# Moving squares of attention probabilities through the device's memory instead of directly between partitions

## The chip, the cores and the metric

The kernel runs on one core of one Trainium2 chip. The metric is the device time of the whole kernel in microseconds (us). The engines are TensorE (PE in the profile, PEld for its weight loads), VectorE (DVE), ScalarE (ACT), GpSimd (POOL) and SyncE (SP), which here only issues transfers. The core has 16 DMA engines.

## The reference

Input is x of 8 x 512 tokens with 128 features, 4096 tokens in all. Three residual steps follow one another: a mixture-of-experts feed-forward, an attention over a memory of 4096 keys, and the same feed-forward again.

```python
x = x + 0.5 * ffn(layernorm(x))       # 8 experts of 176, the best 2 of each token, and a shared one
x = x + attn(layernorm(x))
x = x + 0.5 * ffn(layernorm(x))

# attn (only its first output is used)
q      = h @ Wq.T + bq
scores = q @ memory_keys.T / sqrt(128)        # 4096 tokens x 4096 keys
probs  = softmax(scores)
out    = (probs @ memory_values) @ Wo.T + bo
```

## The kernel before

**Stages.** The first feed-forward takes the time up to about 125 us, the attention from there to about 600 us, the second feed-forward the rest. Each engine has its own program in a fixed order; semaphores alone tie them together.

**Units.** The attention runs over 16 units. A unit is 4 tiles of 128 tokens (512 tokens) against one half of the keys (2048). It is cut into 8 half tiles, each 128 tokens x 1024 keys; the loops call the running number of a half tile H, so that unit u has H = 8u to 8u + 7. For each half tile TensorE computes the scores (`scores`, L1138 to L1140), VectorE their maximum (`maximum`, L909), and ScalarE the exponentials (`exponentials`, L647 or L656).

**Transposing.** The product with the values needs the probabilities transposed, keys on partitions. For one of the 4 tiles of a unit TensorE does this (`transpose_pair`, L1157). The other three (MOVED = 3) are the "moved" tiles: their exponentials are written to the buffer `E2`, VectorE transposes 32 x 32 blocks in place (`transpose_squares`, L904), and DMA carries each square of 32 partitions to the partitions on which it belongs in `probsT`. For a block row b and a source group i of 32 partitions this is one transfer of its own from `E2[i*32:(i+1)*32, ..., b, :]` to `probsT[b*32:(b+1)*32, ...]`. So there are 16 transfers for a batch, and a unit has two batches: tiles 0 and 1 (128 KB each transfer), and tile 2 (64 KB each). `probsT` has two halves, used by turns of units; `E2` has one.

**Splitting and use.** ScalarE copies 768 columns of `probsT` to `p_hi` in fewer bits (`moved_high`, L629), GpSimd subtracts to get `p_lo` (`moved_low`, L423), and TensorE multiplies both with the values (L1178 to L1180). There are 8 such steps ("rings") to a unit. The first `moved_high` of unit u waits until both batches of unit u are in (`moved[0]`, `moved[1]`). In ScalarE's fixed order it stands at H = 8(u + 1) + 2, between the exponentials of half tiles 2 and 3 of unit u + 1.

**Order on SyncE** (L312 to L324). For each unit: wait until the half of `probsT` is free (`moved_lo_done`), then for each batch wait for its transposed squares (`squares_done`) and issue its 16 transfers. The batch of tiles 0 and 1 waits for the squares of half tile 3. VectorE transposes half tile 3 two half tiles later in its own order, after `own_low` (L897) and `maximum` (L909).

**Reuse of E2.** The exponentials of the next unit may write into `E2` only when the batch there has landed (`wait(act, moved[...], moves(u))` in `exponentials`).

Of the kernel before, what the change touches and what calls it, by code (L numbers as in the profile page):

```python
# [4 lines left out]
fp32 = mybir.dt.float32  # L5
# [6 lines left out]
P = 128  # L12
# [4 lines left out]
N = GT * P  # L17
# [24 lines left out]
MOVED = 3  # L42
OWN = GT - MOVED
BATCHES = ((0, 2), (2, 1))
SQ = 32
QUADS = P // SQ
# [26 lines left out]
def macaron_kernel(nc: bass.Bass, x, wup, wdown, gate_w, expert_bias, shared_up, shared_down,  # L73
                   wq, bq, wo, bo, keys_values, out):
    with ExitStack() as ctx:
        def sb(name, shape, dt):
            return ctx.enter_context(nc.sbuf_tensor(name, shape, dt))

        def sem(name):
            return ctx.enter_context(nc.semaphore(name))  # L80
# [31 lines left out]
        E2 = sb("E2", [P, MOVED, QUADS, N], fp32)  # L112
# [12 lines left out]
        probsT = sb("probsT", [P, 2, MOVED * QUADS, KC, SQ], fp32)  # L125
# [22 lines left out]

        p_hi = sb("p_hi", [P, HI_RING, GT * QUADS, 2 * SQ], fp32r)
        p_lo = sb("p_lo", [P, HI_RING, GT * QUADS, 2 * SQ], fp32r)  # L150
        bank_max = sb("bank_max", [P, 2, 2], fp32)
        neg_max = sb("neg_max", [P, 4, GT], fp32)
        row_sum = sb("row_sum", [P, 4, GT, 2], fp32)
# [63 lines left out]
        exp_done = sem("exp_done")  # L217
        probsT_done = sem("probsT_done")
        squares_done = sem("squares_done")
        moved = [sem(f"moved{k}") for k in range(len(BATCHES))]  # L220
        p_hi_done = sem("p_hi_done")
        p_lo_done = sem("p_lo_done")
# [17 lines left out]
        def wait(eng, s, n):  # L240

            if not isinstance(n, int) or n > 0:
                eng.wait_ge(s, n)
# [12 lines left out]
        def score_pair(u, i, h):  # L256

            p = (2 * (u * GT + i) + h) % SCORE_PAIRS
            return banks[:, 2 * p:2 * p + 2, :]
# [17 lines left out]
            return TB[:, 0:2 * OWN * P].rearrange("p (c a q) -> p a c q", c=2, q=SQ)  # L277

        def moves(units):
            return 16 * QUADS * QUADS * units  # L280

        def batch_of(i):
            return [k for k, (first, count) in enumerate(BATCHES) if first <= i < first + count][0]
# [5 lines left out]
        def tiles_of(g):  # L289
            return bass.ds(g * GT, GT)  # L290

        @block.sync
        def _(sp):
            sp.dma_start(X[:, 0:GT, :], x[:, 0:GT, :]).then_inc(x_loaded[0], 16)
            sp.dma_start(wup_f, wup).then_inc(up_w_loaded, 16)
            sp.dma_start(X[:, GT:2 * GT, :], x[:, GT:2 * GT, :]).then_inc(x_loaded[1], 16)
            small = [(sup_s[:, :, :], shared_up), (sdown_s[:, :, :], shared_down), (wq_s[:, :], wq), (bq_s[:, :], bq)]
            for dst, src in small:
                sp.dma_start(dst, src).then_inc(small_w_loaded, 16)
            sp.dma_start(X[:, 2 * GT:3 * GT, :], x[:, 2 * GT:3 * GT, :]).then_inc(x_loaded[2], 16)  # L300
            sp.dma_start(wdown_f, wdown).then_inc(down_w_loaded, 16)
            sp.dma_start(X[:, AHEAD * GT:, :], x[:, AHEAD * GT:, :]).then_inc(x_loaded[AHEAD], 16)
            for b in range(2):
                sp.dma_start(kv_stage[:, b, :], keys_values[:, b, :]).then_inc(kv_loaded[b % 2], 16)
            for dst, src in [(wo_s[:, :], wo), (bo_s[:, :], bo.to_broadcast([P, D]))]:
                sp.dma_start(dst, src).then_inc(out_w_loaded, 16)
            for b in range(2, KV):
                sp.wait_ge(kv_hi_done, b - 1)
                sp.wait_ge(kv_lo_done, b - 1)
                sp.dma_start(kv_stage[:, b % 2, :], keys_values[:, b, :]).then_inc(kv_loaded[b % 2], 16)  # L310

            for u in range(UNITS):  # L312
                if u == 0:
                    sp.wait_ge(z_done, GROUPS)
                    sp.wait_ge(down_done, GROUPS * SLOTS)
                wait(sp, moved_lo_done, UP * (u - 1))
                for k, (first, count) in enumerate(BATCHES):
                    sp.wait_ge(squares_done, 2 * (MOVED * u + first + count))
                    for b in range(QUADS):
                        for i in range(QUADS):  # L320
                            target = probsT[b * SQ:(b + 1) * SQ, u % 2, :, :, :].rearrange(
                                "p (t i) c q -> p i t (c q)", t=MOVED)[:, i, first:first + count, :]
                            sp.dma_start(target, E2[i * SQ:(i + 1) * SQ, first:first + count, b, :]  # L323
                                         ).then_inc(moved[k], 16)  # L324
            for g in range(GROUPS):
                sp.wait_ge(x_updated, GROUPS + g + 1)
                sp.dma_start(out[:, tiles_of(g), :], X[:, tiles_of(g), :]).then_inc(stored, 16)
            sp.wait_ge(stored, 16 * GROUPS)
# [3 lines left out]
        def _(pool):  # L332
# [32 lines left out]
            def spread_weights(G):  # L365

                slots = routed_slots(G)
                T = (slots.stop - slots.start) * GT
                pool.wait_ge(weights_ready, route_event(G) + 1)
                if G == GROUPS:  # L370
                    pool.wait_ge(moved[-1], moves(UNITS))
                if G >= 2:
                    pool.wait_ge(wbc_done, G)
                pool.tensor_copy(wide_weights(G)[:, slots, :].rearrange("p s (m r) -> p (s m) r", r=ROWS),
                                 weight[:, slots, :, :].rearrange("p s t e -> p (s t e)").unsqueeze(2)
                                 .to_broadcast([P, T * E, ROWS])).then_inc(weights_spread, 1)

            def cast_xT(n, G, i):

                pool.wait_ge(xT_copied, n + 1)  # L380
                wait(pool, up_done, SLOTS * (G - AHEAD))
                if G == GROUPS:
                    pool.wait_ge(moved[0], moves(UNITS))
                pool.tensor_copy(xTb[:, i % RING, :], xT[i % RING]).then_inc(xTb_done, 1)
# [99 lines left out]
        def _(act):  # L484
# [138 lines left out]
            def moved_high(ring):  # L623

                if ring % UP == 0:
                    for k in range(len(BATCHES)):
                        act.wait_ge(moved[k], moves(ring // UP + 1))
                wait(act, pv_done, 2 * (ring - HI_RING + 1))
                act.activation(moved_part(p_hi, ring), moved_pair(ring // UP, ring % UP), ACT.Copy  # L629
                               ).then_inc(moved_hi_done, 1)  # L630

            def exponentials(u, i, h):

                v = u % 4
                act.wait_ge(neg_max_done, u * GT + i + 1)
                source = score_pair(u, i, h)
                if u == 0 and i == 0 and h == 0:
                    act.wait_ge(shared_up_done, GROUPS)
                    act.wait_ge(up_done, GROUPS * SLOTS)
                    act.wait_ge(weighted, GROUPS * SLOTS)  # L640
                if i < MOVED:
                    if h == 0:
                        wait(act, moved[batch_of(i)], moves(u))
                        if u == 0 and i == MOVED - 1:
                            act.wait_ge(kv_lo_done, KV)
                    strips = E2[:, i, :, :].rearrange("p b (c q) -> p c b q", q=SQ)
                    act.activation(  # L647
                        strips[:, 2 * h * QUADS:2 * (h + 1) * QUADS, :, :],
                        source.rearrange("p k (c b q) -> p (k c) b q", b=QUADS, q=SQ), ACT.Exp,
                        bias=neg_max[:, v, i:i + 1], accum_out=row_sum[:, v, i, h:h + 1]).then_inc(exp_done, 1)  # L650
                else:
                    if i == MOVED and h == 0:
                        wait(act, probsT_done, (u - 1) * UP)
                        if u < 2:
                            act.wait_ge(ffn_w_cast, 2)
                    act.activation(  # L656
                        probs[:, v % 2, i - MOVED, 2 * h * N:2 * (h + 1) * N],
                        source.rearrange("p b n -> p (b n)"), ACT.Exp,
                        bias=neg_max[:, v, i:i + 1], accum_out=row_sum[:, v, i, h:h + 1]).then_inc(exp_done, 1)
# [22 lines left out]
            for u in range(UNITS + 2):  # L682
                g = u // 2
                prepares = u % 2 == 1 and u < LAST
                for h in range(HALVES):
# [6 lines left out]
                    if u < UNITS:  # L692
                        exponentials(u, h // 2, h % 2)
# [608 lines left out]
```

## Time and profile before

| | us |
|---|---|
| median of 3 runs | 693.62 |
| lowest and highest | 691.54, 698.07 |
| the profiled execution | 697.09 |
| its span, first to last instruction | 695.3 |

| engine | busy us | share of the span |
|---|---|---|
| PE | 617.1 | 89% |
| DVE | 533.2 | 77% |
| ACT | 469.5 | 68% |
| POOL | 392.7 | 56% |

The shares are means over three stages. "SPq" in a row means SyncE's queue of DMA issues, and "issue" as a releaser means that the profile shows nothing the engine waited for. The device's memory was read for 8.12 MB and written for 2.10 MB in the whole run; all DMA together moved 61.17 MB.

### The profile page before, as it was taken

What the parts mean: (1) busy time and instruction counts of PE and PEld (TensorE: products, weight loads), DVE (VectorE), ACT (ScalarE), POOL (GpSimd) and SP (SyncE); (2) the same over time, 40 slices, a digit from 0 to 9 for tenths busy, and PEclk for the clock granted to TensorE, in tenths of its full rate; (3) what the DMA queues carried; (4) which work ended last, traced back from release to release, by engine and by line L of the source; (5) the groups of instructions that cost most, each with busy time, mean ns of one, the idle gap of its engine ahead of it and who ended that gap; (6) DMA issues with size and microseconds to landing.
All of it is one profiled execution on the core that took longest, in us unless ns stands there. A gap on an engine that the chain in (4) does not pass through costs nothing.

```text
span 695.3 us, 9149 instructions
## 1 busy us (share of the span) xinstructions
PE 617.1 (89%) x2768; PEld 429.7 (62%) x2768; DVE 533.2 (77%) x952; ACT 469.5 (68%) x773; POOL 392.7 (56%) x386
## 2 busy tenths in 40 slices
PE   3898979657998998999999999999999858699997
PEld 2544434535876776877777777777777646454542
DVE  3798876866977977888887897896797645188885
ACT  2477979335776776777776777776776644178886
POOL 4755512024765865867766677686687687542200
PEclk9799999988999999999999999999999988899999
DMA  7002010065364453553653644635526530000001
GB/s 286 2 30 62 30 61 0 8 160 124 73 155 95 115 133 86 139 131 77 156 117 74 152 108 104 145 93 127 133 65 149 120 81 0 1 6 26 31 18 44
DMA packets 37092, 61.17 MB, mean 88 GB/s; under 512 B 9051, under 2 KB 9651, under 8 KB 36915
## 3 DMA queue, kind: packets, MB, share of 16 engines
q1 hardware_dynamic: 36755, 60.57, 34.8%
q8 instruction: 23, 0.38, 0.2%
q14 instruction: 26, 0.21, 0.1%
q10 hardware_dynamic: 288, 0.01, 0.0%
HBM read 8.12 MB, written 2.10 MB: 15 GB/s over the span
## 4 chain that ended last, share of the span: by engine, by line
PE 40%; SPq 22%; DVE 14%; issue 11%; POOL 6%; ACT 6%; DMA 1%; ACTq 0%; DVEq 0%; POOLq 0%
SPq L323 22%; PE banks L1021 4%; POOL p_lo L423 4%; PE banks L1030 3%; PE banks L1138 3%; PE banks L1179 3%; PE banks L1140 3%; PE banks L1139 3%; PE banks L1178 3%; PE banks L1180 3%; DVE probsT L810 3%; PE banks L986 3%; DVE bank_max L909 3%; DVE E L904 2%; PE banks L1037 2%
## 5 line engine op out<-in xcount | busy, mean ns | idle before, releaser
L423 POOL TENSOR_TENSOR p_lo<-probsT,p_hi 128x768 fp32r<-128x768 f32 x128 | 235.4, 1842 | 136.3 <-ACT p_hi L629 135.6
L909 DVE TENSOR_REDUCE bank_max<-banks 128x1 f32<-128x1024 f32 x128 | 155.8, 1217 | 36.3 <-PE banks L1140 35.7
L629 ACT ACTIVATE p_hi<-probsT 128x768 fp32r<-128x768 f32 x128 | 107.9, 843 | 30.1 <-issue 27.2
L1138 PE MATMUL banks<-kv_lo,q_parts 128*128 128x512 f32 x256 | 112.5, 440 | 13.6 <-ACT E L647 10.3
L810 DVE SCALAR_TENSOR_TENSOR probsT<-banks,E 128x1024 bf16<-128x1024 f32 x80 | 95.5, 1219 | 35.3 <-PE banks L1021 31.6
L904 DVE STREAM_TRANSPOSE E<-E 128x1024 f32<-128x1024 f32 x96 | 118.4, 1234 | 4.2 <-ACT E L647 4.2
L647 ACT ACTIVATE E<-banks,neg_max 128x1024 f32<-128x1024 f32 x96 | 106.8, 1113 | 20.7 <-DVE neg_max L915 13.4
L531 ACT ACTIVATE probsT<-probsT 128x1024 bf16<-128x1024 bf16 x96 | 92.2, 980 | 31.8 <-DVE probsT L810 22.9
L1178 PE MATMUL banks<-p_hi,kv_lo 128*128 128x512 f32 x256 | 109.3, 427 | 3.9 <-POOL p_lo L423 3.9
L621 ACT ACTIVATE p_hi<-banks 128x256 fp32r<-128x256 f32 x128 | 49.0, 383 | 82.1 <-PE banks L1157 82.0
L1179 PE MATMUL banks<-p_lo,kv_hi 128*128 128x512 f32 x256 | 103.7, 405 | 0.0
L1180 PE MATMUL banks<-p_hi,kv_hi 128*128 128x512 f32 x256 | 103.6, 405 | 0.0
L1140 PE MATMUL banks<-kv_hi,q_parts 128*128 128x512 f32 x256 | 102.1, 399 | 0.0
L1139 PE MATMUL banks<-kv_hi,q_parts 128*128 128x512 f32 x256 | 102.1, 399 | 0.0
L897 DVE TENSOR_TENSOR p_lo<-banks,p_hi 128x256 fp32r<-128x256 f32 x128 | 52.0, 407 | 56.0 <-ACT p_hi L621 55.8
L1138 PEld LDWEIGHTS banks<-kv_lo,q_parts 128*128 128x128 f32 x256 | 49.0, 192 | 22.1 <-ACT E L647 11.8
L1021 PE MATMUL banks<-E,wup_b 128*128 128x512 bf16 x176 | 54.6, 398 | 8.3 <-ACT probsT L520 6.4
L1178 PEld LDWEIGHTS banks<-p_hi,kv_lo 128*128 128x128 f32 x256 | 49.1, 192 | 16.8 <-issue 5.5
L1180 PEld LDWEIGHTS banks<-p_hi,kv_hi 128*128 128x128 f32 x256 | 49.0, 191 | 12.6
L1179 PEld LDWEIGHTS banks<-p_lo,kv_hi 128*128 128x128 f32 x256 | 48.9, 191 | 12.0 <-issue 2.0
L1030 PE MATMUL banks<-probsT,wdown_b 128*128 128x512 bf16 x176 | 52.5, 386 | 4.3 <-ACT probsT L531 4.2
L1140 PEld LDWEIGHTS banks<-kv_hi,q_parts 128*128 128x128 f32 x256 | 48.7, 190 | 11.6
(101 smaller groups left out, 874.8 us busy)
## 6 DMA issues: line engine op xcount, KB each, us to landing
probsT<-E SPq DMA_DIRECT2D x256, 128.0 KB, 2.4
probsT<-E SPq DMA_DIRECT2D x256, 64.0 KB, 2.0
E<-in_keys_values SPq DMA_DIRECT2D x8, 512.0 KB, 3.4
out<-X SPq DMA_DIRECT2D x8, 256.0 KB, 2.1
X<-in_x SPq DMA_DIRECT2D x1, 1280.0 KB, 8.8
X<-in_x SPq DMA_DIRECT2D x3, 256.0 KB, 5.2
probsT<-in_wup SPq DMA_DIRECT2D x1, 704.0 KB, 6.7
probsT<-in_wdown SPq DMA_DIRECT2D x1, 704.0 KB, 6.2
```

The lines of the kernel that those rows point to most:

```text
L323: sp.dma_start(target, E2[i * SQ:(i + 1) * SQ, first:first + count, b, :]).then_inc(moved[k], 16)
L423: pool.tensor_tensor(moved_part(p_lo, ring), moved_pair(ring // UP, ring % UP), moved_part(p_hi, ring).bitcast(fp32), ALU.subtract).then_i ...
L629: act.activation(moved_part(p_hi, ring), moved_pair(ring // UP, ring % UP), ACT.Copy).then_inc(moved_hi_done, 1)
L810: dve.scalar_tensor_tensor(hidden[:, k, :, :], up_banks[PAIR_BANK[k]], 0.0, spread.unsqueeze(1).to_broadcast([P, 2, N]), ALU.max, ALU.mult ...
L904: dve.transpose(half, half).then_inc(squares_done, 1)
L909: dve.tensor_reduce(bank_max[:, i % 2, h:h + 1], score_pair(u, i, h).rearrange("p b n -> p (b n)"), AX.X, ALU.max).then_inc(bank_max_done, 1)
L1138: pe.matmul(bank, qh, kl, start=True, stop=False)
L1139: pe.matmul(bank, ql, kh, start=False, stop=False)
L1140: pe.matmul(bank, qh, kh, start=False, stop=True).then_inc(scores_done, 1)
L1178: pe.matmul(OB, vl, hi, start=(c == 0), stop=False)
L1179: pe.matmul(OB, vh, lo, start=False, stop=False)
L1180: pe.matmul(OB, vh, hi, start=False, stop=(c == KC - 1)).then_inc(pv_done, 1)
```

## The change

Each batch of moved tiles is first written as a whole, from all 128 partitions, to a new tensor `spill` in the device's memory (one transfer of 2 MB or of 1 MB). SyncE waits until it has landed (`spilled`), then issues four transfers back, one for each block row b, which gather the squares of all source partitions into the 32 partitions of `probsT` (512 KB or 256 KB each). `E2` is released when the transfer out has landed, instead of when the squares have arrived. The amount that arrives in `probsT` is the same. Nothing else changes.

```diff
--- before.py
+++ after.py
@@ -148,6 +148,8 @@
 
         p_hi = sb("p_hi", [P, HI_RING, GT * QUADS, 2 * SQ], fp32r)
         p_lo = sb("p_lo", [P, HI_RING, GT * QUADS, 2 * SQ], fp32r)
+
+        spill = nc.dram_tensor("spill", [2, MOVED, P, QUADS * N], fp32, kind="Internal").ap()
         bank_max = sb("bank_max", [P, 2, 2], fp32)
         neg_max = sb("neg_max", [P, 4, GT], fp32)
         row_sum = sb("row_sum", [P, 4, GT, 2], fp32)
@@ -217,6 +219,7 @@
         exp_done = sem("exp_done")
         probsT_done = sem("probsT_done")
         squares_done = sem("squares_done")
+        spilled = [sem(f"spilled{k}") for k in range(len(BATCHES))]
         moved = [sem(f"moved{k}") for k in range(len(BATCHES))]
         p_hi_done = sem("p_hi_done")
         p_lo_done = sem("p_lo_done")
@@ -277,7 +280,7 @@
             return TB[:, 0:2 * OWN * P].rearrange("p (c a q) -> p a c q", c=2, q=SQ)
 
         def moves(units):
-            return 16 * QUADS * QUADS * units
+            return 16 * QUADS * units
 
         def batch_of(i):
             return [k for k, (first, count) in enumerate(BATCHES) if first <= i < first + count][0]
@@ -316,12 +319,15 @@
                 wait(sp, moved_lo_done, UP * (u - 1))
                 for k, (first, count) in enumerate(BATCHES):
                     sp.wait_ge(squares_done, 2 * (MOVED * u + first + count))
+                    wait(sp, moved[k], moves(u - 1))
+                    place = spill[u % 2, first:first + count]
+                    sp.dma_start(place.rearrange("t p n -> p t n"), E2[:, first:first + count, :, :].rearrange(
+                        "p t b n -> p t (b n)")).then_inc(spilled[k], 16)
+                    sp.wait_ge(spilled[k], 16 * (u + 1))
                     for b in range(QUADS):
-                        for i in range(QUADS):
-                            target = probsT[b * SQ:(b + 1) * SQ, u % 2, :, :, :].rearrange(
-                                "p (t i) c q -> p i t (c q)", t=MOVED)[:, i, first:first + count, :]
-                            sp.dma_start(target, E2[i * SQ:(i + 1) * SQ, first:first + count, b, :]
-                                         ).then_inc(moved[k], 16)
+                        sp.dma_start(probsT[b * SQ:(b + 1) * SQ, u % 2, first * QUADS:(first + count) * QUADS, :, :]
+                                     .rearrange("p i c q -> p i (c q)"), place[:, :, b * N:(b + 1) * N].rearrange(
+                            "t (i p) n -> p (t i) n", i=QUADS)).then_inc(moved[k], 16)
             for g in range(GROUPS):
                 sp.wait_ge(x_updated, GROUPS + g + 1)
                 sp.dma_start(out[:, tiles_of(g), :], X[:, tiles_of(g), :]).then_inc(stored, 16)
@@ -640,7 +646,7 @@
                     act.wait_ge(weighted, GROUPS * SLOTS)
                 if i < MOVED:
                     if h == 0:
-                        wait(act, moved[batch_of(i)], moves(u))
+                        wait(act, spilled[batch_of(i)], 16 * u)
                         if u == 0 and i == MOVED - 1:
                             act.wait_ge(kv_lo_done, KV)
                     strips = E2[:, i, :, :].rearrange("p b (c q) -> p c b q", q=SQ)
```

SyncE's program is the place of the change. These are its rows for two units in the middle before, with the semaphores that each row waits for (`probsT<-E` is a direct transfer of squares; x15 counts equal rows):

```order
19 L323 DMA probsT<-E 32x2x512 [waits squares_done]
20 L323 DMA probsT<-E 32x2x512 x15
21 L323 DMA probsT<-E 32x512 [waits squares_done]
22 L323 DMA probsT<-E 32x512 x15
23 L323 DMA probsT<-E 32x2x512 [waits squares_done,moved_lo_done]
24 L323 DMA probsT<-E 32x2x512 x15
25 L323 DMA probsT<-E 32x512 [waits squares_done]
26 L323 DMA probsT<-E 32x512 x15
```

And the same two units of the change:

```order
27 L324 DMA spill<-E 128x2x2048 [waits moved0,squares_done,moved_lo_done]
28 L328 DMA probsT<-spill 32x8x512 [waits spilled0]
29 L328 DMA probsT<-spill 32x8x512 x3
30 L324 DMA spill<-E 128x2048 [waits moved1,squares_done]
31 L328 DMA probsT<-spill 32x4x512 [waits spilled1]
32 L328 DMA probsT<-spill 32x4x512 x3
33 L324 DMA spill<-E 128x2x2048 [waits moved0,squares_done,moved_lo_done]
34 L328 DMA probsT<-spill 32x8x512 [waits spilled0]
35 L328 DMA probsT<-spill 32x8x512 x3
36 L324 DMA spill<-E 128x2048 [waits moved1,squares_done]
37 L328 DMA probsT<-spill 32x4x512 [waits spilled1]
38 L328 DMA probsT<-spill 32x4x512 x3
```

A unit had 32 issues behind two waits for squares; now it has 10, with two more waits in which SyncE sits until its own transfer out has landed.

ScalarE's program is the place that waits for the moved squares. Before, around the first `moved_high` of a unit (L629) and the exponentials of half tile 3 (the second L647), on which the next unit's first batch depends:

```order
173 L621 ACTIVATE p_hi<-banks 128x256 [waits pv_done,probsT_done]
174 L647 ACTIVATE E,row_sum<-banks,neg_max 128x8x4x32 [waits moved0,neg_max_done]
175 L629 ACTIVATE p_hi<-probsT 128x768 [waits pv_done,moved1,moved0]
176 L621 ACTIVATE p_hi<-banks 128x256 [waits pv_done,probsT_done]
177 L647 ACTIVATE E,row_sum<-banks,neg_max 128x8x4x32 [waits neg_max_done]
```

Of the change:

```order
173 L627 ACTIVATE p_hi<-banks 128x256 [waits pv_done,probsT_done]
174 L653 ACTIVATE E,row_sum<-banks,neg_max 128x8x4x32 [waits spilled0,neg_max_done]
175 L635 ACTIVATE p_hi<-probsT 128x768 [waits pv_done,moved1,moved0]
176 L627 ACTIVATE p_hi<-banks 128x256 [waits pv_done,probsT_done]
177 L653 ACTIVATE E,row_sum<-banks,neg_max 128x8x4x32 [waits neg_max_done]
```

No instruction has moved on ScalarE; the wait of the exponentials is now for the transfer out, and that of `moved_high` is the same as before.

## Rows read from the trace of the kernel before

**Rows 1.** The page: busy time of the engines, and the chain that ended last.

```profile
PE 617.1 (89%) x2768; PEld 429.7 (62%) x2768; DVE 533.2 (77%) x952; ACT 469.5 (68%) x773; POOL 392.7 (56%) x386
...
PE 40%; SPq 22%; DVE 14%; issue 11%; POOL 6%; ACT 6%; DMA 1%; ACTq 0%; DVEq 0%; POOLq 0%
```

**Rows 2.** Waits of ScalarE and of SyncE's queue: total us, times, longest.

```profile
ACT p_hi L629 <- issue: 27.2, 15, 3.5
ACT E L647 <- DMA probsT<-E: 7.3, 2, 6.5
...
SPq L318 <- DVE E L904: 120.3, 15, 35.3
```

**Rows 3.** Lines 323 and 629: duration ns min/median/max, first and last start us.

```profile
L323 SPq DMA_DIRECT2D probsT<-E x512: 507/596/2051, 137.1 to 566.8; - x171
...
L629 ACT ACTIVATE p_hi<-probsT x128: 833/843/858, 159.2 to 590.5; 128x768 fp32r<-128x768 f32 x128
```

**Rows 4.** Timeline of SyncE, units 8 and 9: start us, length us, transfers.

```profile
354.55 21.59 SPq L323 DMA_DIRECT2D probsT<-E  x32
...
381.77 21.86 SPq L323 DMA_DIRECT2D probsT<-E  x32
```

**Rows 5.** Timeline of ScalarE and VectorE between them: start, length, [idle before].

```profile
377.65 0.84 ACT L629 ACTIVATE p_hi<-probsT 128x768 fp32r<-128x768 f32 x1 [2.96 <-issue]
378.40 0.36 ACT L621 ACTIVATE p_hi<-banks 128x256 fp32r<-128x256 f32 x1
378.67 1.11 ACT L647 ACTIVATE E<-banks,neg_max 128x1024 f32<-128x1024 f32 x1
...
378.80 0.42 DVE L897 TENSOR_TENSOR p_lo<-banks,p_hi 128x256 fp32r<-128x256 f32 x1 [1.82 <-ACT p_hi L621]
379.14 1.22 DVE L909 TENSOR_REDUCE bank_max<-banks 128x1 f32<-128x1024 f32 x1
380.39 0.16 DVE L915 TENSOR_REDUCE neg_max<-bank_max 128x1 f32<-128x2 f32 x1
380.46 1.24 DVE L904 STREAM_TRANSPOSE E<-E 128x1024 f32<-128x1024 f32 x1
```

**Rows 6.** The same timelines: squares of tile 2, and the last unit's first L629.

```profile
388.68 1.24 DVE L904 STREAM_TRANSPOSE E<-E 128x1024 f32<-128x1024 f32 x1
...
568.89 0.84 ACT L629 ACTIVATE p_hi<-probsT 128x768 fp32r<-128x768 f32 x1 [3.54 <-issue]
```

**Rows 7.** The page's DMA issues: transfers, KB each, median us from issue to landing.

```profile
probsT<-E SPq DMA_DIRECT2D x256, 128.0 KB, 2.4
probsT<-E SPq DMA_DIRECT2D x256, 64.0 KB, 2.0
E<-in_keys_values SPq DMA_DIRECT2D x8, 512.0 KB, 3.4
out<-X SPq DMA_DIRECT2D x8, 256.0 KB, 2.1
```

**Rows 8.** Windows: length, busy us of PE, PEld, DVE, ACT, POOL, PEclk, DMA share, GB/s.

```profile
10.00:13.00 3.00, 2.22 (x10) 1.78 (x8) 0.00 (x0) 1.86 (x2) 2.92 (x7) 1.00 1.04 434
193.00:203.00 10.00, 9.68 (x49) 7.67 (x48) 7.20 (x10) 6.93 (x14) 6.27 (x4) 1.00 0.88 203
204.00:214.00 10.00, 10.00 (x49) 8.03 (x48) 8.33 (x10) 5.91 (x11) 7.37 (x5) 1.00 0.38 95
300.00:518.00 218.00, 211.49 (x991) 164.88 (x990) 181.98 (x286) 157.53 (x287) 154.05 (x113) 1.00 0.49 116
...
693.60:694.60 1.00, 0.00 (x0) 0.00 (x0) 0.00 (x0) 0.00 (x0) 0.00 (x0) 0.59 0.69 262
```

**Rows 9.** Windows of TensorE alone: length, PE busy us, PEclk, DMA share, GB/s.

```profile
144.20:147.60 3.40, 0.69 (x3) 1.00 0.88 204
147.60:151.00 3.40, 0.33 (x1) 0.51 0.63 149
151.00:154.50 3.50, 3.50 (x9) 0.50 0.39 95
...
374.00:378.00 4.00, 3.60 (x17) 1.00 0.33 82
```

**Rows 10.** The page: traffic with the device's memory over the whole run.

```profile
HBM read 8.12 MB, written 2.10 MB: 15 GB/s over the span
```

## The prediction, as it went on record

> **What bounds the kernel now.** I read the page first. TensorE is busy for 89% of the span, but only 40% of the chain that ended last is PE, and 22% is SyncE's queue of issues [rows 1]. That is too much for an engine which computes nothing, so I looked at what releases what.
>
> SyncE issues 512 direct transfers, from 137.1 to 566.8 us, and one issue takes 596 ns [rows 3]. A unit's 32 follow each other in one string of 21.6 us (unit 8) and 21.9 us (unit 9) [rows 4]. The string starts when VectorE has transposed half tile 3; SyncE waits there 15 times [rows 2]. At the other end ScalarE's first `moved_high` of a unit waits for the last square: "issue", 15 times, 27.2 us in sum, up to 3.5 us at once [rows 2]. The profile names no releaser, but the last landing of unit 8 fits: the string ends at 376.1 us, its last transfer was issued some 0.6 us earlier, a 64 KB transfer lands 2.0 us after its issue [rows 4, 7], which is 377.5, and L629 starts at 377.65 [rows 5].
>
> These two waits close a ring, for the exponentials of half tile 3 stand behind that same `moved_high` in ScalarE's order. The timeline shows it [rows 5]: L629 at 377.65, the copy L621, then VectorE's L897, maximum, and the transpose L904 from 380.46 to 381.70; SyncE's next string starts at 381.77 [rows 4]. So a unit costs D + G. D goes from the first issue to L629, 377.65 - 354.55 = 23.1 us. G goes from L629 to the next first issue, 381.77 - 377.65 = 4.12 us. Check: the first issue is at 137.1, the last unit's L629 at 568.89 [rows 3, 6]; 137.1 + 16 x 23.1 + 15 x 4.12 = 568.5. The ring sets the attention's time; what comes before 137.1 and after 568.9 is not touched.
>
> How much other engines leave below it: in 300 to 518 us, eight units, PE is busy for 211.49 of 218.0 us [rows 8]. That is 26.4 us for a unit of 27.25. So a shorter D gives little, a longer D costs its full length in every unit.
>
> **The change, part by part.** It removes 32 issues from D and puts two round trips in their place, one after the other, since SyncE waits for each transfer out itself.
>
> Rates. Loads over 128 partitions moved 434 GB/s with all 16 DMA engines full (share 1.04), 417 GB/s for a share of 1 [rows 8]. Transfers into 32 partitions moved 203 GB/s at a share of 0.88; with no idle engine that is 231 [rows 8]. Each DMA engine is half as fast there: 434 / 1.04 / 16 = 26 GB/s against 203 / 0.88 / 16 = 14.4. The transfers back also end in 32 partitions each, so I take 217, the middle of 203 and 231. That it is the narrow destination and not the narrow source that costs is my choice; no row of before has one without the other (rival 1).
>
> Fixed parts. The 256 KB store lands after 2.1 us [rows 7], of which 0.63 are data at 417 GB/s: 1.5. The 64 KB transfer lands after 2.0, less 0.30 for data at 217: 1.7. The 512 KB load lands after 3.4, less 1.26: 2.1, the upper end for all.
>
> The new D:
> - Out, batch 0: 1.5 + 2.097 MB / 417 GB/s = 1.5 + 5.03 = 6.5 us.
> - Back, batch 0 (four issues, hidden behind the data of the first), with the transfer out of batch 1 queued behind it on the same DMA engines: 1.7 + 9.66 + 2.51 = 13.9 us. Its squares are no hindrance: half tile 5 is transposed at 389.92, 8.2 us after the string's start [rows 4, 6], and SyncE comes to that issue at 6.5 + 4 x 0.64 = 9.1 us.
> - Back, batch 1: 1.7 + 4.83 = 6.5 us.
> - SyncE waking up twice: 0.1 us, a guess.
>
> D = 27.0 us, against 23.1. If the transfer out of batch 1 is not held back by the one before, its fixed part and wait overlap with data, about 1.8 us less.
>
> What is costed at nothing: G, which has no DMA in it; ScalarE's earlier release of `E2` (at 6.5 instead of about 12 us into the unit). The latter removes at most the 7.3 us of two waits [rows 2], and both lie before an L629 that waits anyway. The longer stall is 27.0 + 4.12 - 26.4 = 4.7 us of a unit, in which PE, DVE and POOL run dry; their work, 26.4 us at most, fits into 31.1. SyncE has no other work in this stage, and the transfers that it would delay are the stores of the last stage, from 624 us on.
>
> Sum: 137.1 + 16 x 27.0 + 15 x 4.12 = 630.9 against 568.9: 62.0 us more. The profiled execution took 697.1 us, 3.5 more than the median of 693.6; it would become 759.1, and the median 755.6.
>
> A page's price for the fixed part: the Trainium skill ("DMA: Bandwidth & Descriptors", Anatomy of one DMA) gives about 2.0 us, most of it the receipt of the write, with the device's memory as the slowest target. As an estimate D would be 1.1 us longer by it, and the median 773. The store's 2.1 us in all [rows 7] speak against so much.
>
> **The rivals.**
>
> *Rival 1, faster: the way back runs at full rate.* If the half rate comes from reading 32 partitions, the transfers back read the device's memory and move at 417 GB/s. Then D = 6.5 + (1.7 + 5.03 + 2.51) + (1.7 + 2.51) + 0.1 = 20.1, below the 22.3 at which the other engines (26.4 - 4.12) become the bound. The gain lies between 8 units x 6.5 us of PE idleness, doubled (13 us), and the 27.2 us of rows 2: about 674 us. The switch is at D = 23.1, a rate back of 3.15 MB / 10.8 us = 291 GB/s. For it: the first loads do reach 434. Against it: they spread over 128 partitions; the rate of an engine fell by almost half as soon as a transfer covered 32. Chance 7%. The Trainium skill ("SBUF — State Buffer", Door 1: The DMA port swizzle) says that 32 partitions reach 8 of 16 ports and at most about 218 GB/s, whichever the other side is; the direct transfers' 203 agree. The same page (The DMA setup-cost knee) has 2 us + bytes / 436 GB/s for wide transfers, with the advice to make one large transfer of many; by that alone this rival would hold, at an estimated D of 20.4.
>
> *Rival 2, much slower: pieces of 2 KB from the device's memory.* The way back gathers 2 KB pieces, 8 KB apart from partition to partition and 256 KB from square to square, while 16 engines run in step. Traffic with that memory goes from 8.12 + 2.10 MB [rows 10] to about 111 MB, and rows show it at full rate for 3 us only; one store over 1 us moved 262 GB/s [rows 8]. With 150 GB/s back (a bound I set between the 95 and 203 of rows 8), D is 33.4 and the median 858. For it: nothing in the trace shows such a gather. Against: the loads of x are 2 KB pieces too. Chance 9%. The Trainium skill ("DMA: Bandwidth & Descriptors", Latency and other measured facts) has copies within that memory at 207 GB/s with a row pitch of 512 KiB and at 103 with 4 MiB; whether a pitch of 8 or 256 KB costs anything no run here shows.
>
> *Rival 3, slower by the clock.* Where PE was busy for only 0.69 of 3.4 us, its clock went from 2.4 to 1.2 GHz for the next 6.9 us [rows 9]; the 3 us stall at 374 to 378 us left it at 2.4. A stall of 4.7 us may drop it. At half speed for 6.9 us PE falls behind by at most 3.5 us, less than 4.7: nothing. Only if it stays low for twice as long, it becomes the bound, at 26.4 + 6.9 = 33.3 us a unit: 2.2 x 16 = 35 us more, 791. Chance 5%.
>
> *Rival 4, no change:* fixed parts and rates err together, so that D falls to 22.5 to 23.5. It needs 4 us less than summed. Chance 3%.
>
> **The numbers.** The forecast of 756 us has 76%. Its own bounds: with 231 and 434 GB/s and 1.5 us each time, D is 25.6 and the median 733; with batch 1's way out overlapped as well, some 24 and 708. With 203, 262 (the store) and 2.1 us each, D is 33.8 and the median 864. Not all go one way, so I take somewhat over half the way on either side, 725 to 815; rival 3 lies within, the others outside. A difference of 1% is about what a measurement of this kernel can tell. Faster by over 1%: 7%, rival 1. Within: 3%. Slower: 90%.
>
> **What would show it.** SyncE's rows: 160 issues in the attention, the read back starting 6 to 8 us after the transfer out. Traffic with the memory of 58 MB read and 52 MB written. The DMA rate on the way back near 217 GB/s. L629's idle time before it (now [rows 5] 2.96 us) at 4 to 7 us in each unit, and the first L629 at 164 us instead of 159.2. PE's busy share in mid-attention down from 97% to about 85%. G still at 4.1 us. I am wrong if the transfers back show much over 217 GB/s or batch 1's transfer out lands before the last square of batch 0, if the idle time is not before L629, or if PEclk falls below 1 for most of the stage.

## The result

| | before, us | the change, us | ratio, 95% interval |
|---|---|---|---|
| median of 4 runs each | 694.75 | 804.96 | 1.158 [1.149, 1.167] |
| span of the profiled execution | 695.3 | 805.9 | |

The change costs 110 us. The forecast was 62 us more (756, range 725 to 815): the direction, the place and the mechanism came out, and the rise that was forecast is just over half of the one measured.

### The profile page after: what moved, and what is told of

Its sections match the earlier page's. It is cut to its first block, busy times and chain, and to the rows that moved or that the text cites. A ratio compares the mean times of both kernels' runs of the same rounds, so it can differ in the third digit from the quotient of the medians.

```text
span 805.9 us, 8811 instructions
## 1 busy us (share of the span) xinstructions
PE 644.3 (80%) x2768; PEld 450.7 (56%) x2768; DVE 536.6 (67%) x952; ACT 467.8 (58%) x773; POOL 391.7 (49%) x386
## 4 chain that ended last, share of the span: by engine, by line
DMA 31%; issue 23%; PE 21%; DVE 13%; POOL 6%; ACT 4%; SPq 3%; ACTq 0%; DVEq 0%; POOLq 0%
DMA spill<-E 30%; PE banks L1027 3%; PE banks L1036 3%; DVE probsT L816 3%; DVE bank_max L915 3%; DVE E L910 3%; SPq L328 3%; POOL p_lo L429 2%; PE banks L1043 2%; PE banks L969 2%; PE banks L992 1%; POOL xn L364 1%; PE banks L984 1%; PE banks L1144 1%; PE banks L1145 1%
## 5 line engine op out<-in xcount | busy, mean ns | idle before, releaser
L635 ACT ACTIVATE p_hi<-probsT 128x768 fp32r<-128x768 f32 x128 | 108.0, 843 | 132.7 <-issue 116.9
L1144 PE MATMUL banks<-kv_lo,q_parts 128*128 128x512 f32 x256 | 115.5, 451 | 11.0 <-ACT E L653 7.7
L1184 PE MATMUL banks<-p_hi,kv_lo 128*128 128x512 f32 x256 | 115.3, 451 | 3.9 <-POOL p_lo L429 3.9
L816 DVE SCALAR_TENSOR_TENSOR probsT<-banks,E 128x1024 bf16<-128x1024 f32 x80 | 95.6, 1218 | 33.5 <-PE banks L1027 29.7
L1185 PE MATMUL banks<-p_lo,kv_hi 128*128 128x512 f32 x256 | 108.5, 424 | 0.0
L1186 PE MATMUL banks<-p_hi,kv_hi 128*128 128x512 f32 x256 | 108.0, 422 | 0.0
L1145 PE MATMUL banks<-kv_hi,q_parts 128*128 128x512 f32 x256 | 104.9, 410 | 0.0
L1146 PE MATMUL banks<-kv_hi,q_parts 128*128 128x512 f32 x256 | 104.6, 409 | 0.0
L627 ACT ACTIVATE p_hi<-banks 128x256 fp32r<-128x256 f32 x128 | 48.9, 382 | 91.8 <-PE banks L1163 91.7
L969 PE MATMUL banks<-ident,xn 128*128 128x128 f32 x96 | 20.7, 354 | 91.7 <-DVE p_lo L903 70.2
L1163 PE MATMUL banks<-ident,probs 128*128 128x128 f32 x256 | 52.9, 290 | 28.7 <-DVE p_lo L903 27.1
L969 PEld LDWEIGHTS banks<-ident,xn 128*128 128x128 f32 x96 | 14.4, 179 | 98.9 <-DVE p_lo L903 73.7
L1163 PEld LDWEIGHTS banks<-ident,probs 128*128 128x128 f32 x256 | 36.3, 149 | 54.5 <-DVE p_lo L903 32.5
L1184 PEld LDWEIGHTS banks<-p_hi,kv_lo 128*128 128x128 f32 x256 | 52.9, 207 | 17.8 <-issue 5.6
```

The costliest lines, as they stand in the source:

```text
L816: dve.scalar_tensor_tensor(hidden[:, k, :, :], up_banks[PAIR_BANK[k]], 0.0, spread.unsqueeze(1).to_broadcast([P, 2, N]), ALU.max, ALU.mult ...
L1144: pe.matmul(bank, qh, kl, start=True, stop=False)
L1145: pe.matmul(bank, ql, kh, start=False, stop=False)
L1146: pe.matmul(bank, qh, kh, start=False, stop=True).then_inc(scores_done, 1)
L1184: pe.matmul(OB, vl, hi, start=(c == 0), stop=False)
L1185: pe.matmul(OB, vh, lo, start=False, stop=False)
```

## The profile after, beside that of before

The page of the change, its parts 1 to 4 in extract (compare [rows 1, 10]):

```profile
span 805.9 us, 8811 instructions
...
PE 644.3 (80%) x2768; PEld 450.7 (56%) x2768; DVE 536.6 (67%) x952; ACT 467.8 (58%) x773; POOL 391.7 (49%) x386
...
HBM read 58.45 MB, written 52.43 MB: 138 GB/s over the span
...
DMA 31%; issue 23%; PE 21%; DVE 13%; POOL 6%; ACT 4%; SPq 3%; ACTq 0%; DVEq 0%; POOLq 0%
```

DVE, ACT and POOL are busy as long as before, within 4 us. PE is busy for 27 us more with the same 2768 matmuls, at a lower granted clock (see e5). The chain has changed its owner: SyncE's issues fell from 22% to 3%, and DMA, 1% before, is now 31%. "issue", which is also the releaser that the profile gives for the wait at the end of the ring, grew from 11% to 23%. Now the waits that the change adds, and the one at the end of the ring (compare [rows 2]; total us, times, longest):

```profile
SPq L328 <- DMA spill<-E: 299.9, 32, 13.6
...
ACT p_hi L635 <- issue: 116.9, 15, 10.1
```

SyncE sits for 300 us in the 32 waits for its own transfers out. ScalarE's wait before the first `moved_high` (L629 before, L635 now) grew from 27.2 to 116.9 us in the same 15 units, by 89.7. One unit in the middle shows the whole ring. These are the timelines of SyncE, ScalarE and VectorE for unit 8 (compare [rows 4, 5]):

```profile
408.81 0.38 SPq L324 DMA_DIRECT2D spill<-E  x1
415.22 1.78 SPq L328 DMA_DIRECT2D probsT<-spill  x4
417.10 0.52 SPq L324 DMA_DIRECT2D spill<-E  x1
431.23 1.73 SPq L328 DMA_DIRECT2D probsT<-spill  x4
...
438.94 0.84 ACT L635 ACTIVATE p_hi<-probsT 128x768 fp32r<-128x768 f32 x1 [9.33 <-issue]
439.69 0.36 ACT L627 ACTIVATE p_hi<-banks 128x256 fp32r<-128x256 f32 x1
439.96 1.11 ACT L653 ACTIVATE E<-banks,neg_max 128x1024 f32<-128x1024 f32 x1
...
440.09 0.42 DVE L903 TENSOR_TENSOR p_lo<-banks,p_hi 128x256 fp32r<-128x256 f32 x1 [8.19 <-ACT p_hi L627]
440.43 1.22 DVE L915 TENSOR_REDUCE bank_max<-banks 128x1 f32<-128x1024 f32 x1
...
441.75 1.24 DVE L910 STREAM_TRANSPOSE E<-E 128x1024 f32<-128x1024 f32 x1
```

The stretch from L635 to the end of the transpose (442.99) is the same as before: G is 4.1 us. D is 438.94 - 408.81 = 30.1 us, where it was 23.1. The three legs of D can be read off SyncE's rows: 6.4 us out, 16.0 us back and out again, 7.7 us back. Over the 16 units the means are 6.65, 15.6 and 7.7, in sum 29.9. The same means before were D = 22.8 and G = 4.5, so that unit 8 with its 23.1 and 4.12 is right in the sum and slightly off in both parts.

The ring accounts for the whole: D rose by 7.16 us in 16 units, and the 15 stretches G between them shrank by 0.39, which makes 108.7 us. The last unit's first L635:

```profile
677.62 0.84 ACT L635 ACTIVATE p_hi<-probsT 128x768 fp32r<-128x768 f32 x1 [8.72 <-issue]
```

It came at 568.89 before [rows 6]: 108.7 of the span's 110.6 us have been lost up to there, and the first transfer left at 137.1 before and at 137.2 now.

The DMA landings of the page (KB each, median us; compare [rows 7]):

```profile
spill<-E SPq DMA_DIRECT2D x16, 2048.0 KB, 6.4
probsT<-spill SPq DMA_DIRECT2D x64, 512.0 KB, 8.5
spill<-E SPq DMA_DIRECT2D x16, 1024.0 KB, 13.0
probsT<-spill SPq DMA_DIRECT2D x64, 256.0 KB, 5.1
```

The 2 MB out land in 6.4 us, and the 1 MB out take 13.0: they stand behind the four transfers back. And windows of SyncE's view, which carry only length, granted clock, DMA share and GB/s, for the legs of unit 8 (compare [rows 8]):

```profile
409.70:414.60 4.90, 0.85 1.03 428
416.10:417.10 1.00, 1.00 0.74 160
417.10:425.90 8.80, 1.00 1.02 212
429.30:431.10 1.80, 1.00 0.04 18
432.10:433.60 1.50, 1.00 0.67 156
433.60:436.80 3.20, 0.73 1.05 228
436.80:438.40 1.60, 0.50 0.27 54
```

In full flow the transfers back move 212 to 228 GB/s, and 217 was assumed. But the second and the third leg each start with 1.0 to 1.5 us at some 160, and end with one or two in which few DMA engines still work. In 429.3 to 431.1 the share is 0.04, less than one engine of 16, and SyncE waits for it.

## The experiments

All runs were compared with the kernel before on the same chip, whose medians there were 696.8 to 698.1 us. Runs on different chips are compared by their ratios to it. D and G are means over the 16 units, if no unit is named.

The theory is the ring: the attention takes 16 D + 15 G, with a floor set by the other engines. Its rivals: traffic with the device's memory as such costs time, or TensorE's lower clock does.

**Transfers back to 128 partitions (e1).**

```diff
-  sp.dma_start(probsT[b*SQ:(b+1)*SQ, u % 2, first*QUADS:(first+count)*QUADS, :, :] ...,
-               place[:, :, b*N:(b+1)*N].rearrange("t (i p) n -> p (t i) n", i=QUADS))
+  row = first * QUADS + b * count
+  sp.dma_start(probsT[:, u % 2, row:row + count, :, :] ...,
+               place[:, :, b*N:(b+1)*N].rearrange("t p n -> p t n"))
```

> The changed kernel, but each of the four transfers back of a batch goes from the same bytes of the spill tensor (2 KB pieces, 8 KB apart) to all 128 partitions, in place of 32; the squares arrive in wrong places, the amount is the same. In the changed kernel a unit's D (first issue to first L629) is 29.9 us and the data back of batch 0 move at 193 GB/s. If the 32 partitions at the destination set that rate: back at over 400 GB/s, D = 6.5 + (1.7 + 5.0 + 2.5) + (1.7 + 2.5) = 20 us, the ring falls below the other engines, 675 to 695 us. If gathering 2 KB pieces from the device's memory sets it: still near 193 GB/s, D near 30, 800 to 810 us. If TensorE's lower clock cost the time: it goes with the stall, so this run can't tell it from the first.

Measured: 725.75 us, ratio 1.043 [1.039, 1.048], D 24.5 us. Neither end came. The destination's width is most of it: D fell by 5.4 of the 7.1 us by which the change had raised it, and the time by some 80. But the way back did not reach 400 GB/s. Windows of SyncE's view for unit 8 of this run:

```profile
371.60:375.60 4.00, 1.00 0.79 227
375.60:377.60 2.00, 1.00 1.00 360
```

It began at 227 for 4 us and then ran at 360, which is 271 over these 6 us.

**Direct transfers over 128 partitions (e2).**

```diff
-  for i in range(QUADS): sp.dma_start(<32 partitions b>, E2[i*SQ:(i+1)*SQ, first:first+count, b, :])
+  sp.dma_start(probsT[:, u % 2, row:row + count, :, :] ..., E2[:, first:first + count, b, :])
```

> The kernel before, but a batch goes in four direct transfers over all 128 partitions in place of sixteen over 32 (the same bytes, squares in wrong places). D becomes 8.2 us (squares of tile 2) + 2.6 + 2 = 13 us, so the transfers leave the ring. It shows the floor that the other engines set. By the ring theory 667 to 682 us, no idle time before L629, a unit of 26.0 to 26.6 us in place of 27.3. If the issues of the kernel before were hidden and something else set its unit, 690 to 696 us.

Measured: 671.53 us, ratio 0.964 [0.962, 0.967]. SyncE's eight issues of unit 8 and what ScalarE does at the first `moved_high` (L627 here):

```profile
340.18 8.59 SPq L321 DMA_DIRECT2D probsT<-E  x8
...
360.25 0.84 ACT L627 ACTIVATE p_hi<-probsT 128x768 fp32r<-128x768 f32 x1
```

L627 has no idle time before it, here and in the other units. So 671.5 is the floor that the other engines set, and the kernel before paid some 25 us for its ring, near the upper end of what rival 1 allowed (27.2).

**One batch alone (e3, e4).** The semaphore counts (`moves`) and the waits follow each batch's own way; the other batch keeps its sixteen direct transfers.

```diff
+  if k != WHICH:        # WHICH = 0 in e3, 1 in e4
+      <the sixteen direct transfers of before>
+      continue
```

> Only tiles 0 and 1 go by way of memory; tile 2 goes in sixteen direct transfers as before. Ring theory with the durations of the changed kernel: out 6.4, back until 18.2 us, then 1.05 MB of direct squares at 203 GB/s queued behind it, 5.2 us, and 0.4: D = 23.8 to 24.5 us against 22.8 before, 16 to 27 us more than before, 708 to 722 us. If the slow part is the mere traffic with the memory, two thirds of the change's 110 us stay: 765 to 770.

> Only tile 2 goes by way of memory; tiles 0 and 1 go in sixteen direct transfers. Ring theory: the direct issues end at 10.3 us, transfer out 0.9 + 2.5 + 0.7 to 1.9, back 1.3 + 6.0 + 0.4: D = 22.5 to 23.5 us against 22.8 before, so 688 to 705 us, no change or little. If each batch through memory costs by its bytes, one third of 110 us: 730.

Measured: e3 725.68 us, ratio 1.040 [1.035, 1.046], D 24.6. e4 699.18 us, ratio 1.0031 [1.0005, 1.0056], D 22.7. Two thirds of the bytes alone cost 29 us, one third alone 2 us, both together 110. Traffic as such is refuted, since the price does not go by the bytes. e3 came 4 us above its range. SyncE's rows for unit 8, first of e3, then of e4, tell why both together are dearer:

```profile
366.82 0.38 SPq L332 DMA_DIRECT2D spill<-E  x1
373.23 1.95 SPq L336 DMA_DIRECT2D probsT<-spill  x4
375.23 10.97 SPq L327 DMA_DIRECT2D probsT<-E  x16
```

```profile
352.87 10.21 SPq L327 DMA_DIRECT2D probsT<-E  x16
363.18 0.54 SPq L332 DMA_DIRECT2D spill<-E  x1
368.09 1.85 SPq L336 DMA_DIRECT2D probsT<-spill  x4
```

Each has one wait of SyncE for a transfer out, and in each it follows at once (6.4 and 4.9 us). Only with both does a transfer out stand behind 2 MB of slow transfers back, while SyncE waits 13 us for it.

**TensorE kept busy through the stall (e5).**

```diff
-  for k in range(2):
+  again = 6 if (i, h) == (2, 1) else 0
+  for n, k in enumerate((0,) * again + (0, 1)):     # scores_done only for the last two
```

> The changed kernel, in which TensorE repeats the first bank's three score products of half tile 5 six more times in every unit, 18 matmuls or 4.2 us more work a unit, in the stall before the first L629; the values are the same. In the changed kernel the granted clock is 0.905 in the mean and falls to 1.2 GHz around each stall. If the lower clock cost a part of the 110 us, the clock rises to 0.95 or more and the time falls, by up to 30 us (770 to 790). If only the ring of transfers sets the time, the clock rises, but the time stays at 800 to 812 us, though 67 us of work were added.

Measured: 808.23 us, ratio 1.159 [1.154, 1.164]; the change itself had 1.158. Windows of 300 to 620 us, the changed kernel and then this run (columns as in rows 8):

```profile
300.00:620.00 320.00, 263.90 (x1148) 204.53 (x1149) 215.96 (x339) 183.99 (x336) 178.56 (x133) 0.90 0.67 185
```

```profile
300.00:620.00 320.00, 295.92 (x1328) 230.49 (x1327) 215.53 (x339) 184.47 (x336) 179.90 (x133) 0.97 0.68 187
```

The clock rose from 0.90 to 0.97, PE was busy for 32 us more in this stretch, and the time did not move beyond the interval; D was 29.7 and G 4.2. So the lower clock is a consequence of the stall. That a gain by the clock was just eaten up by the added work is unlikely, as D consists of the transfers and did not change by more than 0.3 us.

**The order of the transfers (e6, e7).**

```diff
+  out_to_memory(0)
+  back(0, (0, 1))
+  out_to_memory(1)
+  back(0, (2, 3))       # e7: issued by ScalarE, at the end of the unit, instead
+  back(1, range(QUADS))
```

> The changed kernel with the transfer out of batch 1 issued after the first two transfers back of batch 0, not after all four. By the changed kernel's durations: out 6.4; two back until 12.8; out of batch 1 until 16.1 and landed by 18.0; the other two back until about 21; back of batch 1, queued behind them, 5.8 us and 0.4: D = 26.5 to 27.5 us in place of 29.9, 38 to 54 us less: 750 to 768 us. If the order of the transfers did not matter, since the bytes are the same and the DMA engines are the limit, 800 to 810.

> As the run before, but the last two transfers back of batch 0 (to partitions 64 to 127) are issued by ScalarE on its own queue, beside SyncE's two (to partitions 0 to 63). If the 32 partitions at the destination limit a transfer and transfers to other partitions can run beside it, data move at over 300 GB/s where the two queues overlap and D is 24 to 25.5 us, 710 to 735 us. If the DMA engines serve them one after the other, D is 26.5 to 27.5 and the time that of the run before, 750 to 768 us, plus up to 1.2 us a unit of issues on ScalarE.

Measured: e6 757.2 us, ratio 1.086 [1.080, 1.092]; D is 26.8 and G 4.1. The same bytes in another order save 48 us, as the legs said. e7 759.11 us, ratio 1.086 [1.079, 1.093]: no gain from the second queue. Its timelines for unit 8, then the queues in 399.5 to 403 us (packets, MB, share of 16 engines; q1 is SyncE's, q10 ScalarE's):

```profile
391.73 0.40 SPq L325 DMA_DIRECT2D spill<-E  x1
...
394.74 0.31 ACTq L682 DMA_DIRECT2D probsT<-spill  x1
395.07 0.56 ACTq L682 DMA_DIRECT2D probsT<-spill  x1
```

```profile
q10 hardware_dynamic: 371, 0.73, 98.9%
q1 hardware_dynamic: 21, 0.07, 4.7%
```

ScalarE issued at 394.7 and 395.1, behind the transfer out of 391.7. No data of its queue moved before 399, when that was nearly done. The queues hardly overlapped, so whether transfers to different partitions could run side by side was not tested after all; only that a second queue did not get it here.

**Contiguous reads (e9, e10), and older data (e11).** e9 and e10 read one contiguous quarter of the batch for each transfer back, to 32 and to 128 partitions; e11 is e1 reading the half of `spill` that was written a unit earlier.

```diff
-  place[:, :, b*N:(b+1)*N].rearrange("t (i p) n -> p (t i) n", i=QUADS)
+  quarter.rearrange("(p i n) -> p i n", p=SQ, n=N)          # e9; p=P in e10
+  older = spill[(u + 1) % 2 if u else 0, first:first + count]   # e11, in e1's place
+  wait(sp, moved[k], moves(u))          # e11, before each transfer out; moves(u - 1) in the change
```

> The changed kernel, but each transfer back reads one contiguous quarter of the batch in the spill tensor, 16 KB or 8 KB for each of its 32 partitions, in place of 2 KB pieces gathered at pitches of 8 KB and 256 KB; the squares arrive in wrong places, the amount is the same. In the changed kernel data come back at 193 GB/s in batch 0 and 180 in batch 1, and 2 KB pieces to 128 partitions at 275. If the 32 partitions are the limit and the pieces cost a little beside it: 200 to 220 GB/s, D 27.5 to 29.3 us, 770 to 797 us. If the pieces are the limit: over 275 GB/s, D under 26 us, under 745 us. If neither matters to the other, 800 to 810.

> As the run before, but to 128 partitions: contiguous reads of 4 KB or 2 KB for each partition, in four transfers a batch. With gathered 2 KB pieces this took 725.75 us at a D of 24.5 us. If the gather in the device's memory held it at 275 GB/s, it now reaches over 380, D is 21 to 22.5 us and the ring is at the other engines' floor: 672 to 692 us. If data just written come back slowly however they are read, the rate stays near 275 and the time at 715 to 730 us.

> The run with gathered 2 KB pieces to 128 partitions (725.75 us, D 24.5 us), but from the half of the spill tensor that was written one unit before, not the one just written; the values are wrong, the amount and all waits are the same. There the first 3 to 4 us of each way back ran at 210 to 300 GB/s and the rest at 370 to 406. If data just written come back slowly, the slow start goes: 2.1 MB at about 390 GB/s take 5.4 us in place of 7.6, batch 1 gains about 1 us, D 21 to 22 us, 675 to 695 us. If every start of a read from the memory is slow, or the bank pattern is at fault, 718 to 732 us as before.

Measured: e9 779.47 us, ratio 1.121 [1.114, 1.129], D 28.5. e10 721.18, ratio 1.036 [1.027, 1.044], D 24.4. e11 724.84, ratio 1.040, D 24.5. Into 32 partitions the gather of 2 KB pieces costs 1.4 of 29.9 us of D. Into 128 it makes no clear difference against e1, and neither does the age of the data. The waits of e11 are not quite the same, as the last line of its edit shows: SyncE also waits for the squares of the unit before, which have landed by then, since the ring itself waited for them. D does not tell all, though. Windows of SyncE's view for unit 8 of e10:

```profile
373.90:377.00 3.10, 1.00 1.09 354
373.90:378.00 4.10, 1.00 0.96 308
```

The contiguous reads begin faster than e1's 227, then fall off, and the legs end as late. The way back from memory stays below the rate of the way out in its mean, and I have not found the cause.

**A faster version (e8, e12).** SyncE's string of issues is the bound of the kernel before, so a part of batch 1's direct transfers goes to ScalarE's queue.

```diff
-  for b in range(QUADS):
+  for b in range(QUADS - k):              # e12: QUADS - 2 * k
...
+  if u < UNITS and h == HALVES - 1:       # ScalarE, end of a unit
+      act.wait_ge(squares_done, 2 * (MOVED * u + first + count))
+      <the transfers of b = 3; e12: of b = 2 and 3>
```

> The kernel before (all transfers direct), with the last four of batch 1's sixteen issued by ScalarE at the end of the unit in place of SyncE. Ring theory: SyncE's string is four issues of 0.64 us shorter, D falls from 22.8 to about 20.3 us, below the floor of the other engines; ScalarE has room for some 2 us of issues a unit. 672 to 686 us. If issues on ScalarE delay its exponentials on the chain, 690 us or more.

> All transfers direct, with eight of batch 1's sixteen issued by ScalarE in place of four (with four: 681.5 us, D 21.0 us, with the floor of the wide direct transfers at 671.5). SyncE's string is 2.5 us shorter again, and leaves the ring; ScalarE has about 2 us more issues a unit. If the ring still cost what is left to the floor: 672 to 678 us. If ScalarE's issues cost it: 682 to 695.

Measured: e8 681.46 us, ratio 0.977 [0.972, 0.981]: faster than both kernels, by 1.9 to 2.8% against the one before, and by the ratios some 9 us above the floor of e2. D is 21.0, and the waits before L629 fell to 6.3 us. e12 710.93, ratio 1.022 [1.015, 1.030]: worse than leaving it alone, and outside both ranges expected. Timeline of ScalarE in e12, unit 8:

```profile
369.86 0.84 ACT L629 ACTIVATE p_hi<-probsT 128x768 fp32r<-128x768 f32 x1
369.94 5.53 ACTq L671 DMA_DIRECT2D probsT<-E  x6
375.56 0.38 ACT L621 ACTIVATE p_hi<-banks 128x256 fp32r<-128x256 f32 x1 [4.86 <-issue]
375.85 1.11 ACT L647 ACTIVATE E<-banks,neg_max 128x1024 f32<-128x1024 f32 x1
```

Its data instructions stand still for 4.86 us while six issues run. The first two issues of the eight ran beside its data instructions; the other six took 0.9 us each and did not. TensorE is short of work: in 300 to 518 us PE is busy for 204.4 us in e12 and for 215.5 in e8.

## Why the prediction came out as it did

- *The ring, its two ends and G.* Right. SyncE waits for the transpose, ScalarE for the last square, and G stayed at 4.1 us through every stalled unit. e6 moved D alone and the time followed. In e3 and e4, nearer to the floor, the time followed D too, with G at 4.2 and 4.7 against 4.5 before.
- *The part outside costs nothing.* Right: about 2 us of 110 arose after the last first-L635.
- *First leg, 6.5 us.* Measured 6.65. The rate of 417 (428 measured) and the fixed 1.5 us from a 256 KB store held for 2 MB. The 2.0 us named beside the sum, which the Trainium skill ("DMA: Bandwidth & Descriptors", Anatomy of one DMA) gives for transfers issued by GpSimd, are not borne out in this leg of SyncE's: it took 6.4 us in all, most often.
- *Second leg, 13.9 us.* Measured 15.6. This is the first mis-sized term, 1.7 us too small. The assumed 217 GB/s were right in full flow (212), but bytes divided by a steady rate leave out the start and the tail. The transfer out of batch 1 was given 2.5 us, and in unit 8 its last engine came one to two us after the rest; from unit to unit this leg varied between 14.9 and 16.2 us.
- *Third leg, 6.5 us.* Measured 7.7, 1.2 us too small in the sum, in the same way: data for nearly 6 us, where 4.8 were summed.
- Together 2.9 us a unit, 16 times: 46 of the 48 us between 62 and 110; the other 2 arose outside the ring. The fixed part was taken from single, short transfers; that the skew between the 16 engines doesn't show there is my reading, and no run tested it. That 805 lies in the range is in part luck: its upper bound stood on lower rates (203 and 262 GB/s), and the rates came as assumed. With 2.1 us for each fixed part, the highest considered, the second and third legs would still have been summed too short. Some of the working is slightly off as well, without effect on the forecast: the switch of rival 1 comes out at 297 GB/s instead of 291, the lower bound of D at 25.5 instead of 25.6.
- *Rival 1, full rate back.* Its premise, a narrow source as the cause of the half rate, fails for the way back: that reads no partitions at all and moved 212 in full flow, and with the same source e1 shows the destination's 32 partitions to be most of it. The rule of the Trainium skill ("SBUF — State Buffer", Door 1: The DMA port swizzle) that 32 partitions give at most about 218 GB/s agrees with the 212 here; the 228 in the full flow of the third leg are 5% above it. But the step behind the rival, that over 128 partitions the way back would move 417 and end at 674 us, failed as well: 725.
- *Rival 2, the gather.* Real but small beside 32 partitions: 1.4 us of D (e9), nothing clear over 128.
- *Rival 3, the clock.* The clock fell around the stall of every unit, and that cost nothing (e5), as argued: the loss stays inside the stall. One row was misread there: in 374 to 378 us ScalarE waited for 3 us, but PE was busy for 3.60 of 4.0 [rows 9], so that the row tells nothing of a stall of PE. For unit 8, windows of TensorE alone (columns as in rows 9):

```profile
430.00:434.00 4.00, 2.52 (x12) 1.00 0.36 95
434.00:438.00 4.00, 0.00 (x0) 0.64 0.84 171
438.00:442.00 4.00, 1.43 (x6) 0.50 0.00 1
```

PE was idle from 434 to 438 us; the clock went from 2.4 to 1.2 GHz in it and stayed low past the stall's end.

- *The signs.* The 160 issues, the 58 MB read and 52 MB written, the first read back 6.4 us after the transfer out and G at 4.1 came as forecast. Others went past their bounds, in the direction of the two legs that were too short: the idle time before L635 was 7.8 us in the mean (4 to 7 forecast), the first L635 came at 166.8 us (164), and PE was busy for 82% of mid-attention (85%). The clock was 0.90 there in the mean, which is 1.2 GHz for a fifth of the time and 2.4 for the rest, so not below full for most of the stage.

## What to carry to other kernels

When a queue's issue time bounds a ring, count the new chain of transfers leg by leg, each to its last landing, before trading many issues for few: fewer issues gained nothing here, since the first two of the three legs ended in a wait of the issuing queue, and a short transfer stood behind a long slow one. To each leg add what it takes beyond bytes over rate: here 1.6 us for the leg that was one transfer out with nothing before it, 3.4 and 2.9 us for the two with transfers back to 32 partitions. If only issue time is short, hand a few issues to another queue that has room, and stop well before its own work stands still.

## What the runs showed of the hardware that was not expected

- Reads from the device's memory to 128 partitions averaged 271 GB/s over 6 us (e1), against 428 for the writes of the change. Gather, contiguous rows and data one unit old gave the same times. Reads from that memory are not slow as such: the first loads of the kernel before are reads too and moved 434 [rows 8]. What makes the difference stays open.
- In unit 8 the last of the 16 DMA engines finished the 1 MB transfer out, which stood behind four others, one to two us after the rest (share 0.04 for 1.8 us).
- ScalarE's transfers (e7) got no data moved until SyncE's, issued earlier, were nearly through (issue at 394.7, no data before 399).
- None of these runs has a source of 32 partitions with a destination of 128, so the price of a narrow source by itself stays open.
